# Expert weights of a mixture-of-experts layer moved in 2048-byte packets in place of 6144 and 4096 bytes

## The reference

```python
probs = softmax(x @ gate_w.T); w, sel = top_k(probs, 8); w = w / sum(w)
# xin[e, slot] = x[tok]: up to 128 tokens for each of 64 experts
h = silu(einsum("ech,ehi->eci", inp, wg)) * einsum("ech,ehi->eci", inp, wu)   # 512 -> 192, twice
out = einsum("eci,eih->ech", h, wd)                                           # 192 -> 512
y = zeros((T, 512)).at[tok].add(g)     # g: the rows of out, weighted
```

## Time and profile before

| | |
|---|---|
| median of 3 runs | 1709.13 us (1702.77 to 1710.74) |
| the profiled execution, its own time | 1722.31 us |
| its span | 1720.5 us |
| mean granted clock of PE in it | 0.938 |
| expert phase, first transpose to the last scatter landed | 1349.5 to 1696.5 us |
| last four DMAs | 1696.5 to 1720.5 us |

### The profile page before, as it was taken

How to read it: one execution, slowest core, us unless ns; L and a number is a source line. 1 busy time by engine, 2 the same in 40 slices (tenths; PEclk the granted TensorE clock), 3 DMA queues, 4 the chain that set the end, 5 groups by cost and what they waited for, 6 DMA issues and landing times. The chain is left out here.

```text
span 1720.5 us, 18848 instructions
## 1 busy us (share of the span) xinstructions
PE 1505.0 (87%) x5792; PEld 1038.6 (60%) x5792; DVE 1049.3 (61%) x1535; ACT 587.0 (34%) x1050; POOL 784.6 (46%) x483
## 2 busy tenths in 40 slices
PE   6989966899857999888999989999985699999990
PEld 2444323577645777776787878888874355555550
DVE  4887679798789887889888865452454122222220
ACT  4444633343534244534333332121321133233220
POOL 3467854253744345634445434773257322222232
PEclk8999987999978999999999999999997799999995
DMA  6899764256663666667565557998761599999997
GB/s 205 247 281 266 213 199 163 73 157 190 202 180 126 187 205 213 188 202 268 154 186 186 173 166 248 369 370 256 241 211 54 174 327 324 321 317 311 305 252 135
DMA packets 193539, 380.39 MB, mean 221 GB/s; under 512 B 20994, under 2 KB 95106, under 8 KB 192944
## 3 DMA queue, kind: packets, MB, share of 16 engines
q1 hardware_dynamic: 165360, 322.89, 59.7%
q0 software_dynamic: 20032, 39.92, 9.8%
q10 hardware_dynamic: 8064, 16.55, 2.8%
HBM read 301.65 MB, written 124.35 MB: 248 GB/s over the span
## 5 line engine op out<-in xcount | busy, mean ns | idle before, releaser
L1518 POOL TENSOR_TENSOR y<-y,hc 128x2048 f32<-128x2048 f32 x64 | 293.1, 4579 | 255.5 <-DVE hc L1350 255.5
L598 PE MATMUL bank<-tokT,ring 128*128 128x512 f32 x768 | 309.1, 402 | 13.9 <-DVE xall L1202 7.2
L1332 DVE TENSOR_TENSOR_SCAN bx<-bank,state,bx 128x512 f32<-128x512 f32 x256 | 312.7, 1267 | 0.8
L600 PE MATMUL bank<-tokT,ring 128*128 128x512 f32 x768 | 303.7, 395 | 0.0
L599 PE MATMUL bank<-tokT,ring 128*128 128x512 f32 x768 | 303.4, 395 | 0.0
L975 ACT ACTIVATE bank<-dl,an 128x512 f32<-128x512 f32 x256 | 171.0, 684 | 330.6 <-DVE bx L1332 330.5
L1524 POOL TENSOR_TENSOR act<-th,act 128x512 fp32r<-128x512 f32 x88 | 116.0, 1318 | 260.3 <-ACT act L899 259.7
L854 PE MATMUL bank<-wgu,xeT 128*128 128x384 f32 x512 | 178.5, 492 | 5.9 <-DMA wde<-wd_in 4.5
L598 PEld LDWEIGHTS bank<-tokT,ring 128*128 128x128 f32 x768 | 146.8, 191 | 50.6 <-issue 17.6
L600 PEld LDWEIGHTS bank<-tokT,ring 128*128 128x128 f32 x768 | 146.7, 191 | 32.4
L610 PE MATMUL bank<-ring,act 128*128 128x512 f32 x352 | 143.7, 408 | 24.7 <-DVE th L1182 19.4
(11 more groups left out here) (151 smaller groups left out, 2106.3 us busy)
## 6 DMA issues: line engine op xcount, KB each, us to landing
ring<-w_all SPq DMA_DIRECT2D x286, 512.0 KB
wgu<-wgu_in SPq DMA_DIRECT2D x64, 768.0 KB
wde<-wd_in SPq DMA_DIRECT2D x64, 384.0 KB
slots<-empty_in SPq DMA_DIRECT2D x16, 1154.0 KB, 8.8
w_all<-staged_u SPq DMA_DIRECT2D x64, 256.0 KB, 3.1
xe<-slots ACTq DMA_DIRECT2D x56, 288.5 KB
w_all<-fst SPq DMA_DIRECT2D x48, 256.0 KB, 3.8
w_all<-staged_d SPq DMA_DIRECT2D x32, 256.0 KB, 3.8
```

The costliest lines, as they stand in the source:

```text
L598: nc.tensor.matmul(b[:, :], w[:, k, 0, :], x[:, 0, k, :], start=(k == 0), stop=False)
L600: last = nc.tensor.matmul(b[:, :], w[:, k, 1, :], x[:, 0, k, :], start=False, stop=(k == KT - 1))
L1332: nc.vector.tensor_tensor_scan(bx[:, k, :], dA[k % 2][:, :], bx[:, k, :], state[:, k, n:n + 1], ALU.mult, ALU.add).then_inc(S_sc, 1)
L1518: nc.gpsimd.tensor_tensor(y[c % 2][:, :, :], y[c % 2][:, :, :], hc[:, :, :], ALU.add).then_inc(S_ya, 1)
```

## The change

Both weight loads get a limit on the length of a contiguous piece: 512 floats, 2048 bytes. The DMA's shape goes from 128x1536 to 128x3x512 for `wgu` and from 96x1024 to 96x2x512 for `wde`. Bytes, addresses, order, semaphores and waits are as before, on every engine; the loads of the first eight experts, which stand in the drain, are changed too. For each engine and expert, q1 has 24 + 12 packets with data in place of 8 + 6.

```diff
                     def load_weights(e, i):
                         if not isinstance(e, int):
                             sp.wait_ge(S_gm, e - DEEP + 1)
-                        sp.dma_start(wgu[i][:, :, :], a["wgu"].rearrange("e p k f -> (e p) k f")[ds(e * P, P), :, :]).then_inc(S_ew[i], 16)
+                        sp.dma_start(wgu[i][:, :, :], a["wgu"].rearrange("e p k f -> (e p) k f")[ds(e * P, P), :, :],
+                                     max_dma_last_dim=D * 4).then_inc(S_ew[i], 16)
                         if not isinstance(e, int):
                             sp.wait_ge(S_y, e - DEEP + 1)
-                        sp.dma_start(wde[i][:, :, :], a["wd"].rearrange("e p s h -> (e p) s h")[ds(e * FH, FH), :, :]).then_inc(S_ew[i], 16)
+                        sp.dma_start(wde[i][:, :, :], a["wd"].rearrange("e p s h -> (e p) s h")[ds(e * FH, FH), :, :],
+                                     max_dma_last_dim=D * 4).then_inc(S_ew[i], 16)
```

## The result

The changed kernel takes 1735.5 us (median of 22 runs, 1711.65 to 1747.13), the kernel before 1710.71 us (22 runs, 1699.38 to 1721.57). The ratio is 1.0117, 95% interval 1.0094 to 1.0139, about +20 us. Eight of the changed kernel's 22 runs were more than 1.5% above its own fastest and are left out of the ratio, none of before's; the medians of all runs are 25 us apart (1.0145).

What follows compares the result with a forecast made beforehand. PE, busy 87%, was taken to bound the kernel, with late scatters at its end and DMA engines full in the expert phase. +8.9 + 6 - 9.4 + 0.5 = +6 us on 1709.13 gave 1715 us, range 1697 to 1731.

Steps and rivals of the forecast that it cites:

- second rival: Expert phase: small packets get less through beside scatters, leaving more reading at the low rate; 1731 us, chance 0.16.
- Step 1: Expert phase: each scatter waits 1.4 to 1.6 us less; 6.4 scatters move ahead, last weights come 8.9 us later.
- Step 2: Weight loads of the last 56 experts: cost of the additional packets on the engines, +6 us, between 0 and 13.6.
- Step 3: End of the expert phase: fewer late scatters, so 16.1 us behind the last weights, not 25.5; 9.4 us less.
- Step 4: SP's issue: a queue full sooner costs nothing; early loads in the drain delay `ring` loads, +0.5 us, 0 to 2.
- Memory did not recover: Rival for the expert phase: small packets read faster, 0.3 us for an expert comes back; 1692 us, chance 0.22.
- the change does nothing for the scatters: Rival for the expert phase: scatters stay as late, 8.4 behind the last weights, only packet cost remains; 1716 us, chance 0.20.

## Why the prediction came out as it did

I forecast no change to slightly slower, 1715 us, 1697 to 1731. On the predicted base of 1709.13 us a ratio of 1.0117 is 1729 us: inside the range near its end. With the medians of all runs (1.0145) it would be 1734 us, just outside. Either way it is my second rival, priced at 1731 us with a chance of 0.16, and not the forecast: +20 to +25 us where my sum had +6. The range held only because that rival had set its upper end.

*Step 1, the wait of a scatter: right in the main.* From issue to landing a scatter takes 8.8 to 9.0 us (median) all through the phase of the changed kernel, as forecast. In the second profile of before it took 9.9 us between 70 and 130 us from the start of the phase and 10.6 us in the 90 us behind that, so the gain is 0.9 us at first and 1.7 later (forecast 1.4 to 1.6). The period is another matter. Timeline of POOL in the changed kernel:

```profile
1404.32 1.54 POOL L1654 DMA_INDIRECT acc<-ye,tok  x1 [4.67 <-DMA acc<-ye,tok]
...
1424.98 1.54 POOL L1654 DMA_INDIRECT acc<-ye,tok  x1 [5.50 <-DMA acc<-ye,tok]
...
1464.79 1.55 POOL L1654 DMA_INDIRECT acc<-ye,tok  x1 [5.44 <-DMA acc<-ye,tok]
...
1574.18 1.54 POOL L1654 DMA_INDIRECT acc<-ye,tok  x1 [4.37 <-ACT ye L1132]
...
1586.43 1.54 POOL L1654 DMA_INDIRECT acc<-ye,tok  x1 [4.52 <-ACT ye L1132]
```

Up to 1465 us one scatter waits for the one before it, and the six periods from 1404.32 us are 10.1 us on average (forecast 9.8; before 10.7 to 10.8 at the same stage and 11.3 later). After that POOL waits for ACT, that is for the rows that PE is late with, and the period is 12.2 us, longer than before's: the scatters no longer pace anything. I had written that 4.9 us for an expert was just PE's pace; PE, short of weights, fell to 6.1.

The scatters moved ahead of the last weights were 4.7 and not 6.4, some 6.5 us in place of 8.9, and the debt was 3.7 and not about 2.

*Step 2, the packets: the term that failed.* I took +6 us, between 0 and 13.6. q1's end came 33 us later, counted from the start of the phase (354 - 321; on the clock of the trace before that is 1704 us, past the 1695 that I had named as the sign of slower). Of these 6.5 are the scatters, so the term was about +27 us. q1's time for an expert, 4.17 us, is outside the 3.5 to 3.8 named there too. I had looked for a price of the packet itself. The pair without scatters shows that full engines lose no throughput by it. The sum in step 2 held the mix of queues to be as before, though step 1 had just changed it. Beside a scatter the packets pass at about their own pace (97 ns for a small one of q1 and 176 ns for one of q0 from 1500.2 to 1501.5 us), and each slow q0 packet now has a fast partner of a third of the size: 276 GB/s in place of 323. And the scatters, sooner done, leave 0.59 of the time and not 0.42 without them, where the rate was 308 GB/s before and 296 after. Together 0.41 x 276 + 0.59 x 296 = 288 GB/s against 0.58 x 323 + 0.42 x 308 = 317. Of these 29 GB/s the fall beside scatters is the larger part, 19 to 27; the greater share of time without them is worth only 3 at the old rates (0.41 x 323 + 0.59 x 308 = 314). The fall from 308 to 296 makes up the rest; it has no cause that the runs show. The engines are full both times, so the 9% are lost to q1. The rival's sum has this fall beside scatters (1.6 MB of q1 and q10 in 6.3 us, then 0.9 in 5), and I gave it too little weight. A trace in which all packets were large couldn't tell the rate with small ones, so the forecast and this rival should have shared their chance.

In the same step I wrote that without scatters the engines wait for memory. No run shows what they wait for; what the runs show is the low rate itself.

*Step 3, the end: right.* From q1's end to the last four DMAs it is 14.8 us (1689.0 to 1703.8) against 25.5: 10.7 less, forecast 9.4. 33 - 10.7 = 22 us, the difference of the phases.

*Step 4, the issue.* SP blocks on weight loads from 1402 us on in the changed kernel (1401.65 us: 1.45 us), from 1571 us on before, and it fills the chain of waits there. The engines stand at 1.08 all the same. The runs give no sign that this costs anything. Without scatters SP blocked for over 1 us on 31 weight loads with small packets and on one with large, the first at 1530 and 1623 us, and from 1500 to 1600 us both moved the same. With halved scatters it blocked as often as in the changed kernel (63 and 60 loads), and q1's end still came back by 14 us. No run changed the queue alone. For the drain, starts of the phase at 1333.2 to 1343.1 us with small early loads and 1332.8 to 1349.5 us with large ones show no difference.

*The other rivals.* Memory did not recover: q1's time for an expert rose from 3.50 to 4.17 us, and it had to fall under 3.3. That the change does nothing for the scatters is out by step 1. The estimate that I made from the rule of the Trainium skill ("DMA: Bandwidth & Descriptors", "Why small descriptors are slow (HBM only)": about 3 cycles for a packet; 3.5 ns, 4.3 us in all) and mine from the rows (13.6 us) were both about something that is too small for the +27 us. The 0.31 us of q1's time for 22 more packets in the pair without scatters are 14 ns each, as in the rows, with overlap in them.

## What to carry to other kernels

When several DMA queues keep the engines full and pass one packet each in turn, as q1 and q0 do here, the size of a queue's packets is its weight in the turn: making them smaller gives time to the others. Here it went to a queue whose accumulating packets are the slowest for their bytes, and reading in large packets beside them was what filled the engines. In such a balance look at the rate over all queues in each mix, not at one queue's wait or one packet's price; a chain of waits that shortens (10.7 us off the end) says nothing of what is paid before it.

## What the runs showed that I had not expected

- Without scatters, the engines moved 282 GB/s from 1400 to 1600 us, reading weights and rows, with packets of 6144 and 4096 bytes and with 2048 alike. The rate wasn't low from the start: with large packets it was 298 GB/s at a share of 0.94 up to 1460 us, and 276 at 1.03 from 1500 us. What changes there no run shows. 256 bytes of padding, another layout and a 9 MB source in place of 72 MB did not lift the kernels with scatters. Other loads ran at 388 and 422 GB/s. The cause is open. A stretch of the changed kernel with q1 alone, to be held against the earlier trace rows, 1510.8 to 1512.8 us:

```profile
DMA packets 240, 0.46 MB, mean 231 GB/s; under 512 B 14, under 2 KB 14, under 8 KB 240
...
q1 hardware_dynamic: 240, 0.46, 108.8%
```

  261 GB/s with large packets, 231 here, in one stretch of 2 to 3 us each; the size of the packets is no way out of it.
- With a third queue that writes the total was higher: before's kernel moved 323 GB/s beside scatters and 308 without, and the kernel with scatters left out 276 with full engines.
- An accumulating packet of 1024 bytes took 101 ns and one of 2048 bytes 176 ns: some 26 ns for the packet and 75 ns for 1024 bytes, where a load takes 42 ns for as many at its best pace (half of 84.5).
